# A graph attention layer on one core: the query products move to even steps and the ranks into the projection's PSUM bank

## The reference

```python
h = jnp.maximum(_layernorm(x, axis=-1), 0.0)
q = (h @ Wq + bq).reshape(b, m, 8, 64)        # k, v likewise
scores = einsum('bmhd,bnhd->bhmn', q, k) / 8 + transpose(edge_bias[edges], (0, 3, 1, 2))
scores = leaky_relu(scores, 0.2)
scores = where(edges > 0, scores, -1e9)
attn = softmax(scores, axis=-1)
out = einsum('bhmn,bnhd->bmhd', attn, v).reshape(b, m, 512) @ Wp + bp
x = x + out
```

## Time and profile before

| | |
|---|---|
| median of 3 runs | 1009.78 us (1006.59 to 1010.27) |
| the profiled execution | 1007.57 us, its span 1005.8 us |
| TensorE busy (matmul / weight loads) | 962.8 us / 932.7 us |
| VectorE, ScalarE, GpSimd busy | 894.8, 771.6, 518.1 us |
| mean granted TensorE clock | 0.989 of full speed |

### The profile page before, as it was taken

The page is one execution under the profiler, slowest core; times in us unless marked ns, Lnnn a source line. Parts: engine busy times, 40 slices in busy tenths (PEclk is TensorE's granted clock), DMA queues, the critical chain, the costliest instruction groups (busy, mean ns, idle before and its releaser), DMA issues. The chain is left out here.

```text
span 1005.8 us, 28199 instructions
## 1 busy us (share of the span) xinstructions
PE 962.8 (96%) x8652; PEld 932.7 (93%) x8652; DVE 894.8 (89%) x3276; ACT 771.6 (77%) x1732; POOL 518.1 (52%) x955
## 2 busy tenths in 40 slices
PE   5889999999999999999999999999999999999995
PEld 4789999999999999999999999999999999999994
DVE  6699899998999989998899989999899998998983
ACT  5678887787787787788777787778778778778752
POOL 2144554755556555565456455475555655445454
PEclk9889999999999999999999999999999999999998
DMA  5434554445544455445554455444544445544331
GB/s 157 127 84 129 146 147 130 138 118 158 137 128 125 140 151 146 116 121 144 152 143 122 127 149 143 129 133 127 159 125 137 125 138 143 143 118 131 101 81 30
DMA packets 212662, 130.65 MB, mean 130 GB/s; under 512 B 38736, under 2 KB 203100, under 8 KB 212508
## 3 DMA queue, kind: packets, MB, share of 16 engines
q1 hardware_dynamic: 211716, 128.24, 46.9%
q10 hardware_dynamic: 792, 0.53, 0.2%
HBM read 71.83 MB, written 39.85 MB: 111 GB/s over the span
## 5 line engine op out<-in xcount | busy, mean ns | idle before, releaser
L1052 POOL TENSOR_SCALAR a_line<-w,a_bias 128x256 f32<-128x256 f32 x512 | 262.0, 512 | 423.2 <-DVE w L1763 378.6
L1267 PE MATMUL bank<-pt,nat_sb 128*65 128x128 f32 x2048 | 266.3, 273 | 0.3
L1740 DVE CUSTOM_DVE_ANT_0 w<-bank,mask_rows 128x256 f32<-128x256 f32 x512 | 195.8, 419 | 62.2 <-issue 54.1
L1524 ACT ACTIVATE pt<-bank 128x512 f32<-128x512 f32 x256 | 154.5, 603 | 105.7 <-PE bank L1215 99.4
L1763 DVE SCALAR_TENSOR_TENSOR w<-w,shift,a_line 128x256 f32<-128x256 f32 x512 | 230.6, 490 | 2.2 <-POOL a_line L1052 2.0
L1267 PEld LDWEIGHTS bank<-pt,nat_sb 128*65 128x65 f32 x2048 | 231.6, 138 | 0.8 <-issue 0.8
L1752 DVE TENSOR_TENSOR onehot<-val,counts_to 128x512 fp32r<-128x512 f32 x256 | 176.3, 689 | 2.3
L1506 ACT ACTIVATE mask_own<-bank,mask_bias 128x512 bf16<-128x512 f32 x256 | 176.7, 691 | 0.4 <-PE bank L1244 0.4
L1515 ACT ACTIVATE t_sb<-bank 128x512 fp32r<-128x512 f32 x256 | 152.0, 594 | 5.8 <-PE bank L1230 5.6
L1215 PE MATMUL bank<-ident,w 128*128 128x128 f32 x1024 | 154.4, 273 | 0.0
L1204 PE MATMUL bank<-t_sb,q_hi 128*128 128x256 f32 x512 | 142.7, 301 | 3.0 <-DVE wmax L1740 1.5
(11 more groups left out here) (136 smaller groups left out, 1618.0 us busy)
## 6 DMA issues: line engine op xcount, KB each, us to landing
adj_in<-in_adj_dram SPq DMA_DIRECT2D x64, 512.0 KB, 3.9
mask_store<-mask_own SPq DMA_DIRECT2D x64, 512.0 KB, 3.2
mask_rows<-mask_store SPq DMA_DIRECT2D x512, 64.0 KB, 2.4
o_pairs<-o_turned SPq DMA_DIRECT2D x128, 128.0 KB
stack_store<-h_stack SPq DMA_DIRECT2D x8, 512.0 KB, 3.6
x_rows<-in_x_dram SPq DMA_DIRECT2D x8, 256.0 KB, 5.9
x_res<-in_x_dram SPq DMA_DIRECT2D x16, 128.0 KB, 2.2
out_dram<-x_res SPq DMA_DIRECT2D x16, 128.0 KB, 2.1
```

The source lines that it names most:

```text
L1052: nc.gpsimd.tensor_scalar(a_line[:, i % 2, :], w[:, i, :], 5.0, a_bias[:, i:i + 1], ALU.mult, ALU.add)\
L1267: last = pe.matmul(o_part[0:D + 1, P * u:P * u + P], nat_sb[:, t % 2, p % 4 * 2 + u, k, :], pt[:, p % 2, u, k, :], start=(k == 0), stop=(k ...
L1524: nc.scalar.activation(pt[:, p % 2], turned_bank[:, :].rearrange("p (u k r) -> p u k r", u=2, k=2), ACT.Exp, scale=0.8).then_inc(probs_rea ...
L1740: nc.vector.tensor_tensor_reduce(w[:, i, :], row_bank[:, SLOTS * u:SLOTS * u + SLOTS], mask_rows[:, t % 2, p % 4 * 2 + u, :], 0.25, LEAST_ ...
```

## The change

The constants move the query products one step earlier (`QFILL` 9 to 8, so rests 0 and 2 instead of 1 and 3, with `low_q` at rests 1 and 3), and `beta`, the column sums and the mean's product one step later (all to rest 3). The pieces of the row normalization that VectorE does move to rest 2 (`CENTER` 18, `VARIANCE` 22, `NORMED` 30, `LOW` 34), the turning of the new rows to steps of rest 3 (`TURN_H` 35 and 39). The ranks go into columns 448 to 511 of `adj_bank`, and `rank` runs ahead of the projection's half 1 in the same step, which then needs no wait of its own. Functions used once at the start get the bank `misc` as an argument.

```diff
-    MASK, MASK_OUT, MASK_IN, TFILL, QFILL, BETA, COLSUM, VEC = 10, 14, 15, 13, 9, 14, 18, 26
+    MASK, MASK_OUT, MASK_IN, TFILL, QFILL, BETA, COLSUM, VEC = 10, 14, 15, 13, 8, 15, 19, 27
...
-    X_LOAD, CENTER, SQUARES, VARIANCE, RSTD, NORMED, HIGH, LOW, TURN_H, STORE_H = 8, 19, 20, 21, 23, 29, 30, 31, 34, 39
+    X_LOAD, CENTER, SQUARES, VARIANCE, RSTD, NORMED, HIGH, LOW, TURN_H, STORE_H = 8, 18, 19, 22, 23, 30, 31, 34, 35, 40
...
-        o_part, nat_bank, adj_bank, q_bank = turn_banks[0][:, 0:256], turn_banks[1], o_bank, misc
+        o_part, nat_bank, adj_bank = turn_banks[0][:, 0:256], turn_banks[1], o_bank
+        ranks = adj_bank[:, 448:512]
...
@@ adj_bank_uses, q_bank_uses @@
                     yield proj_taken, 2 * (TPG * b + due[0]) + due[1] + 1
-
-            def q_bank_uses(b, s):
                 t = tile(b, s, RANK)
                 if t is not None:
                     yield val_ready, TPG * b + t + 1
+
+            def q_bank_uses(b, s):
...
-            def rank(b, t, s):
+            def rank(b, t, s, dst=ranks):
                 pe.wait_ge(used_ready, TPG * b + t + 1)
-                free(q_bank_uses, b, s, 0)
-                pe.matmul(q_bank[:, 0:TPG * GPT], lower[:, :], used[:, t % 2, :], start=True, stop=True)\
+                free(adj_bank_uses, b, s, 0)
+                pe.matmul(dst[:, 0:TPG * GPT], lower[:, :], used[:, t % 2, :], start=True, stop=True)\
                     .then_inc(rank_done, 1)
...
                 pe.wait_ge(o_moved[t % 2], 48 * (n // 2) + 48)
-                free(adj_bank_uses, b, s, 0)
+                if e == 0 or tile(b, s, RANK) is None:
+                    free(adj_bank_uses, b, s, 0)
...
                     count(b, t, s)
+                t = tile(b, s, RANK)
+                if t is not None and not first(b, t):
+                    rank(b, t, s)
                 due = piece(b, s, PROJ, 2)
                 if due is not None:
                     project(b, *due, s)
                 i = 0
-                t = tile(b, s, RANK)
-                if t is not None and not first(b, t):
-                    rank(b, t, s)
-                    i += 1
...
-            def take_ranks(b, t):
+            def take_ranks(b, t, src=ranks):
...
-                nc.vector.tensor_tensor_reduce(val[:, t % 2, :], q_bank[:, 0:TPG * GPT], used[:, t % 2, :], 1.0, 0.0,
+                nc.vector.tensor_tensor_reduce(val[:, t % 2, :], src[:, 0:TPG * GPT], used[:, t % 2, :], 1.0, 0.0,
```

More of the change, by code:

```diff
@@ L1403, in _ @@
             turn_adj(0, 0, 0)
-            rank(0, 0, 0)
+            rank(0, 0, 0, misc)
             pe.wait_ge(weights_in, 16 * 6)
@@ L1889, in _ @@
             nc.vector.reciprocal(row_rstd[:, tiles_of(0)], row_std[:, tiles_of(0)]).then_inc(rstd_ready, 1)
-            take_ranks(0, 0)
+            take_ranks(0, 0, misc)
             mark(0, 0, 0)
```

## The result

The changed kernel takes 1033.87 us (median of 4 runs, 1029.77 to 1039.04), the kernel before, run beside it, 1008.57 us (1006.59 to 1010.27). The ratio is 1.025, 95% interval 1.0225 to 1.028: slower by 2.5%, where the forecast was +0.3% with a range that ended at 1025. The profiled execution is the 1039.04 us one, the slowest of the four.

What follows compares the result with a forecast made beforehand. TensorE was taken to set the time, VectorE close behind. Waits of 32.5 us come and 29 go: 3.5 us more, 1011.1 us on the profiled execution, put at 1012 as the median; range 999 to 1025.

Steps and rivals of the forecast that it cites:

- point 3: At rest 0, GpSimd's conversion lies over VectorE's x_res, delaying the rank 0.14 us in two tiles a graph: 2 us.
- point 5: Row pieces at rest 2, column sums and new rows at rest 3, low parts at rest 1: no cost.
- Waits that go: TensorE's waits before rank (14 us), projection (10.5), query products behind beta (2.3) and turning (2.2) vanish: 29 us.
- Point 1: At rest 1 the adjacency's turning waits for the ranks behind the low parts, 0.29 us in 57 tiles: 17 us.
- Point 2: Query products at rest 0 wait for VectorE's reading of beta, about 0.7 us twice a graph: 11 us.
- point 4: GpSimd's constant addition after the conversion, twice a graph, may delay x_res: 0 to 7 us, taken as 2.5.
- slower rival: Conversion holds x_res in all tiles (8 us), constant's addition twice a graph (7 us): +14 us, 1023; chance 0.32.
- Point 6: At the start, the wait moves from the rank of step 24 to the turning of step 25: no net change, 3 us either way.
- clock rival: One 3.5 us step a graph at the lower 1.2 GHz clock: 26 us more, 1038; chance 0.02.

Runs made afterwards that it cites:

- e5: The kernel before with only the ranks moved into the projection's bank, ahead of the projection's half 1, all lags as before; 1015.37 us.
- e3: The changed kernel with GpSimd's conversion one step earlier, at rest 3 (CONV 4 to 3); 1023.31 us.
- g2: e1 with the row pieces CENTER and SQUARES moved from steps 18 and 19 to 14 and 15; 1019.52 us.
- h3: g1 with the row pieces CENTER and SQUARES four steps earlier, at steps 10 and 11; 996.16 us.
- e1: The changed kernel with the ranks taken ahead of the low query parts in VectorE's step; 1028.63 us.
- e2: The changed kernel with beta read on VectorE ahead of shift_neg and the mark instead of behind shift; 1033.90 us.
- e7: The changed kernel with VectorE's wait for the masks at rest 1 moved from the maxima to the leaky relu ahead of them; 1028.81 us.
- e4: The changed kernel with three edits: ranks ahead of the low parts, beta read first, GpSimd's conversion at rest 3; 1003.47 us.
- g1: e4 with the row pieces CENTER and SQUARES moved from steps 18 and 19 to 14 and 15; 992.99 us.
- h1: g2 with GpSimd's conversion one step earlier, at rest 3; 998.03 us.
- e8: The changed kernel with GpSimd's sum over heads one step later, at rest 3 (SUM 34 to 35); 1033.11 us.

## Why the prediction was wrong

It summed to 1011.1 us for the profiled execution, which came at 1039.0: 27.9 us short. (By medians, 1033.87 for 1012: 21.9 short.) The step that failed is point 3 with the ground it stood on in point 5: that VectorE reaches rest 0 0.6 us ahead of TensorE, because the row pieces and `shift` at rest 2 cost nothing. The terms, over the seven graphs of steps 32 to 255 where nothing else is said:

- **Waits that go, 29 us.** The size is right, the reason for the largest is not. Rank, projection, query products and turning had 28.8 us together by the account of the kernel before, and the waits of the projection and of the query products at their old places did go. But I booked the rank's 14 us as gone with their cause, the low part, and called the rank free with 0.1 us to spare; in e5, with the low part no longer in its way, it waits 13.6 us for `o_all`.
- **Point 1, the turning: right in mechanism, small in size.** 0.42 us in each of 56 tiles, 23.0 us, for 0.29 and 17. 0.11 of the difference is the second waiting instruction ahead of the first maximum, for the masks, which only rest 1 has; I had read the 0.89 at rest 0, where there is none. +6.0.
- **Point 2, beta: right.** 0.755 us in step 16 and 1.08 in step 24 of a graph, 12.8 us for 10.3, the seven graphs' share of my 11. +2.5.
- **Point 3, the conversion over `x_res`: the step that failed.** "Two tiles of a graph; 2 us", and with point 4 4.5 us; measured 19.4 us of waits before the rank: 0.90 in step 0 of a graph, 0.72 in step 4, 0.28 to 0.42 in steps 12, 20, 24, 28, none in 8 and 16. The condition of the slower rival (that the second leaky relu of rest 0 ends later than 0.1 us before TensorE's step) holds in step 132 (the relu ends 0.89 us after the step's start) and, by the medians over the graphs, in all eight tiles (0.01 us before to 1.18 after), and `x_res` is over 0.5 us and the rank waits in six of the eight; the price, which I had at 0.14 from a `x_res` of 0.59 us, was up to the whole conversion. What I missed is where VectorE entered rest 3: I counted it as on time, while the sums over heads had held `shift` at rest 2 (0.69 for 0.28 us) and the row pieces, which point 5 put at nothing, stood there too (0.96 us in step 130); it began the leaky relu of rest 3 0.79 us into the step. The four tiles behind a row piece hold 15.6 of the 19.4 us. e3 shows the collision's share directly (19.4 to 4.9), and g2 and h3 show the rank's wait moving with a row piece; the share of the pieces ahead of steps 0 and 4 alone is read from the trace, not tried. +15.
- **Point 4, the constant's addition: nothing.** In step 136 of the changed kernel `x_res` took 0.36 us and the rank didn't wait. It is in the sum above.
- **Point 5, at nothing: wrong in its cover.** "0.7 us to spare" at rests 2 and 3 was read from durations of before, and the same operations took longer once they lay elsewhere (42 us in the span). Most of what that cost stands under point 3. The column sums wait 0.28 us in six graphs. +1.7.
- **Point 6, the start: wrong, in part by the clock of this one execution.** Step 32 begins 7.9 us later. The waits at the turnings of steps 21 and 25 (the longest 2.5 us) and for beta (1.3) are there, but they only take the place of what the kernel before had in these steps (2.28 us and a slow step): 7.7 of the 7.9 us are there when step 21 starts. The loads of step 18 show where they came from, in the changed kernel and in e1:

```profile
43.42 0.33 PEld L1206 LDWEIGHTS bank<-t_sb,q_lo 128*128 128x128 f32 x1
43.64 0.33 PEld L1205 LDWEIGHTS bank<-t_sb,q_hi 128*128 128x128 f32 x1
```

```profile
39.72 0.19 PEld L1206 LDWEIGHTS bank<-t_sb,q_lo 128*128 128x128 f32 x1
39.84 0.19 PEld L1205 LDWEIGHTS bank<-t_sb,q_hi 128*128 128x128 f32 x1
```

Loads 0.33 us long and 0.21 apart are what the kernel before shows where its granted clock reads 0.51 (44 to 54 us), the lower level; the changed kernel has them up to 61 us in this execution. In e2, e3 and e7, which keep the low parts ahead of the ranks and whose steps 17 and 18 ran at 0.11 apart, step 32 begins at 96.8 to 97.2. So some 3.7 of the 7.9 us are the clock of this execution, and about 4 the kernel's. Both starts ran slow in places, so the split is rough. +7.9.

Together +33 us, for a miss of 27.9: some 5 us come back. In the kernels with the rank ahead of the projection the time of steps 32 to 255 is that much below what the waits say, against before (changed: waits +28.6, time +23.6; e5, with the old table: +13.1, +7.6). The trace shows where: in the kernel before, the load behind the rank's starts 0.13 us after it (513.11 to 513.24 in the earlier trace rows), in the changed kernel 0.03 or less (487.83 to 487.86); over the 56 tiles that is 7.4 us against 1.4.

- **The clock rival (0.02)** played no part in the changed kernel past its start (1.00 from 62 us to 1017). Its mechanism is real all the same, as e1, e4 and g2 show, at 1.3 us a step and not 3.5. The Trainium skill, TensorE: Matmul & The Clock Gate, section A second HAM failure mode, has short and frequent idle times between groups of products as such a cause. The traces agree only in part: g1 against e4 shows one wait a graph ahead of a drop, while h1, with waits behind beta no shorter than those of g2 and no drop, shows that a wait alone does not decide it.

The slower rival, given 0.32, was the right one by its first mechanism, the conversion over `x_res`; its second, the constant's addition, brought nothing, and its size, 1023, was too small for the same reasons.

## What to carry to other kernels

Where two engines are nearly balanced, a wait of the one is often the lateness of the other: opening it sends the lateness to the next meeting, and only taking work or collisions out of the late engine's chain makes time. So follow the late engine round a whole period with the durations of the new neighbours before calling any wait gone, and try such edits in pairs: here two edits that gave 14 (ranks first, with the row pieces moved) and 11 us alone gave 36 together. And before a difference in the start is put down to the kernel, look at the clock there: it differs between executions. An instruction that is moved takes with it the question of what the other user of its port is doing at the new place.

## What the runs showed of the hardware that I had not expected

- A VectorE operation on 128x4 values, 0.15 us alone, took 0.69 beside GpSimd's additions, and one on 128x64 took 1.12 us instead of 0.25 when a GpSimd conversion of 1.04 us began with it; both end with GpSimd's instruction. Moving GpSimd's work away brought them to 163 ns (e8) and 273 to 311 ns (e3, e4) in the mean. The Trainium skill, SBUF — State Buffer, section Who interferes with whom, calls the shared ports "an exclusive lock", and these runs agree. A row piece on 128x512 values took 0.96 us beside the same sums (L1657, 480.16) and 0.69 without. Not every operation is held: `o_all`, which reads one input from PSUM, took 0.41 to 0.42 us in all 37 cases in which it began inside a GpSimd instruction of the changed kernel, as elsewhere. `onehot` was not lengthened at 478.75, but there it began 0.10 us ahead of the sum; one that began 0.20 us behind a conversion (9.44 us) took 1.38 us.
- A waiting instruction whose semaphore has long come costs VectorE 0.11 us ahead of the maxima (e7: the first maximum starts 0.89 us into most steps of rest 1 instead of 1.00, and the step went from 3.57 to 3.46).
- Eight products of the column sums behind a wait of 0.6 us brought the granted clock from 1.00 to 0.55 for a whole step; with the wait at 0.28 us (changed kernel, e3) or gone (g1) it stayed at 1.00.
